# A four-layer transformer kernel on one core: a new order of work, and planned waits of TensorE filled to their full length

## The reference

```
L0  self attention over 1024 keys with rope and a mask, cross attention with a key mask, MLP with tanh-gelu
L1  self attention over 1024 keys, cross attention, MLP with tanh-gelu
L2  self attention in windows of 128 tokens, shifted by 64; cross attention over the 16 largest scores
    of each query (top-k); MLP with silu(a) * b
L3  self attention with rope, cross attention with rope, MLP with erf-gelu
```

## Time and profile before

| | us |
|---|---|
| median of 3 executions | 2982.82 |
| lowest, highest | 2969.13, 2983.83 |
| profiled execution, its own time | 2987.84 |
| span of the profiled execution | 2985.6 |
| TensorE busy | 2766.4 (93%) |
| VectorE busy | 1892.3 (63%) |
| ScalarE busy | 1421.3 (48%) |
| GpSimd busy | 714.7 (24%) |
| mean granted TensorE clock | 0.967 |

### The profile page before, as it was taken

How to read it: one execution, slowest core, us unless ns; L and a number is a source line. 1 busy time by engine, 2 the same in 40 slices (tenths; PEclk the granted TensorE clock), 3 DMA queues, 4 the chain that set the end, 5 groups by cost and what they waited for, 6 DMA issues and landing times.

```text
span 2985.6 us, 47850 instructions
## 1 busy us (share of the span) xinstructions
PE 2766.4 (93%) x15193; PEld 1377.7 (46%) x15249; DVE 1892.3 (63%) x4177; ACT 1421.3 (48%) x2579; POOL 714.7 (24%) x1063
## 2 busy tenths in 40 slices
PE   8999999999979998899988797899899999999899
PEld 5333444335535324344454565656554423324466
DVE  6887287642664882865554568667976684885621
ACT  3345535563433773566644343323124375676441
POOL 2101001131331110331224355533331000111420
PEclk9999999999989999999998898999899999999899
DMA  6252123322460322332166525531321232123631
GB/s 188 61 149 58 60 74 106 89 74 90 155 191 16 106 56 65 94 114 71 40 186 174 148 71 150 153 96 53 111 72 48 68 90 51 37 59 98 183 100 37
DMA packets 268153, 286.79 MB, mean 96 GB/s; under 512 B 70665, under 2 KB 207243, under 8 KB 267275
## 3 DMA queue, kind: packets, MB, share of 16 engines
q1 hardware_dynamic: 256651, 282.28, 32.3%
q0 software_dynamic: 11264, 1.46, 0.3%
HBM read 167.43 MB, written 114.72 MB: 95 GB/s over the span
## 4 chain that ended last, share of the span: by engine, by line
PE 69%; DVE 12%; DMA 9%; issue 5%; POOL 2%; SPq 2%; ACT 1%; DVEq 0%; ACTq 0%; POOLq 0%
PE ring_b L1420 11%; PE ring_c L1453 11%; PE ring_a L1376 10%; PE ring_b L1476 7%; PE ring_a L1488 7%; PE ring_b L1419 3%; PE ring_b L1333 3%; PE ring_a L1465 3%; DVE row_max L1739 2%; PE ring_a L1476 2%; DMA reciprocals<-scr_recip 2%; PE ring_b L1447 1%; DMA scr_out<-out_stage 1%; PE ring_a L1348 1%; PE ring_b L1408 1%
## 5 line engine op out<-in xcount | busy, mean ns | idle before, releaser
L1561 ACT ACTIVATE probs<-ring_b 128x512 f32<-128x512 f32 (+1 forms) x1728 | 919.2, 599 | 443.8 <-PE ring_b L1420 355.4
L1739 DVE TENSOR_REDUCE row_max<-ring_a 128x1 f32<-128x1024 f32 x512 | 602.0, 1218 | 178.5 <-PE ring_a L1376 177.7
L1420 PE MATMUL ring_b<-q_ring,k_ring 100*128 100x512 bf16 x1536 | 528.1, 381 | 15.0 <-ACT probs L1561 2.0
L1376 PE MATMUL ring_a<-k_ring,q_ring 96*128 96x512 bf16 x1536 | 452.9, 382 | 23.3 <-DVE row_max L1739 11.2
L1453 PE MATMUL ring_c<-probs,v_and_ones 128*17 128x512 f32 x3072 | 400.9, 598 | 2.3 <-ACT probs L1561 1.8
L1852 POOL CAST neg_max_parts<-neg_max 16x128 bf16<-16x128 f32 x112 | 35.6, 318 | 1344.9 <-ACT neg_max L1555 1142.9
L1736 DVE CUSTOM_DVE_ANT_0 w_mlp<-ring_a,w_mlp 128x1024 bf16<-128x1024 f32 x256 | 304.7, 1222 | 53.0 <-PE ring_a L1376 50.7
L1420 PEld LDWEIGHTS ring_b<-q_ring,k_ring 100*128 100x128 bf16 x1536 | 145.7, 97 | 347.9 <-issue 235.7
L1376 PEld LDWEIGHTS ring_a<-k_ring,q_ring 96*128 96x128 bf16 x1536 | 136.1, 98 | 252.3 <-issue 148.8
L1476 PE MATMUL ring_b<-h_feat,w_mlp 128*128 128x512 f32 x512 | 232.1, 600 | 4.1 <-issue 4.0
L1488 PE MATMUL ring_a<-w_mlp 128*128 128x256 f32 x1024 | 225.5, 380 | 2.1 <-issue 0.8
(11 more groups left out here) (144 smaller groups left out, 3514.8 us busy)
## 6 DMA issues: line engine op xcount, KB each, us to landing
q_ring<-scr_q SPq DMA_DIRECT2D x128, 384.0 KB, 4.3
scr_q<-split SPq DMA_DIRECT2D x64, 384.0 KB, 2.6
k_ring<-scr_k SPq DMA_DIRECT2D x64, 384.0 KB, 5.3
scr_q<-split SPq DMA_DIRECT2D x64, 256.0 KB, 3.0
scr_out<-out_stage SPq DMA_DIRECT2D x128, 128.0 KB, 2.4
scr_out<-out_stage SPq DMA_DIRECT2D x64, 256.0 KB, 2.7
h_feat<-scr_out SPq DMA_DIRECT2D x56, 256.0 KB
reciprocals<-scr_recip SPq DMA_DIRECT2D x56, 256.0 KB
```

The source lines that it names most:

```text
L1376: last = mm(ps[:, half * BLOCK:(half + 1) * BLOCK], q[0:PARTS, h, t * P:(t + 1) * P], k_view(g)[0:PARTS, h, half * BLOCK:(half + 1) * BLOC ...
L1420: last = mm(ps[:, :], k_view(g)[0:ROWS, h, s.kt * P:(s.kt + 1) * P], q[0:ROWS, h, q0:q0 + BLOCK], start=not g.masked, stop=True)
L1561: f(PT[0:n, s.pt, :], ps[0:n, :], ACT.Exp, **kw).then_inc(b_evac, 1)
L1739: v.tensor_reduce(NM[:, s.nm, s.u:s.u + 1], ps, AX.X, ALU.max).then_inc(a_evac, 1)
```

## The change

Four things in the planner change, nothing in the code that computes.

First, the ranks, REACH, DELAY, SECOND and LATER have other numbers, so that all five engines issue their steps in another order. Second, transfers are modelled otherwise: each has a time `dma` for its bytes, these queue on one line in the order of issue, and `lat` comes on top of it. Third, some durations are other ones: 2.1 for 1.7 us for the products with values in windows, 1.42 for 1.0 for the inverse root, 0.2 us more for the maxima's transfers. Fourth, fills take the whole planned wait and begin at 0.4 us of it instead of 0.8.

```diff
-            if rest > 0.8:
-                s["fill"] = int((rest - 0.3) * 0.7 / FILL_ONE)
+            if rest > 0.4:
+                s["fill"] = int(rest / FILL_ONE)
...
-            s["fill_o"], s["fill_on"], s["fill_ring"] = int((gap - 0.15) * 0.8 / FILL_ONE), self.count.get(o, 0), o
+            s["fill_o"], s["fill_on"], s["fill_ring"] = int(gap / FILL_ONE), self.count.get(o, 0), o
...
+        if "dma" in s:
+            self.line = max(self.line, at) + s["dma"]
+            end = max(end, self.line)
...
-    out=(0.9, -9, -8.6, -8.6),
+    out=(-12, -10, -8, -12),
...
-DELAY = (7.5, 20)
+DELAY = (7.5, 40)
...
-            s = yield do("root", [("POOL", 1.0)], after=[s], counts=["root_n"], l=l, i=i, b=b, blk=blk, of=s)
+            s = yield do("root", [("POOL", 1.42)], after=[s], counts=["root_n"], l=l, i=i, b=b, blk=blk, of=s)
...
-            s = yield do("load", [("SP", (0.9 if g.edge else 0.38) if cross else 0.82)], after=wr + [q_last, k_last], lat=4.6 if cross else 5.6, g=g, wr=wr,
+            s = yield do("load", [("SP", (0.9 if g.edge else 0.38) if cross else 0.82)], after=wr + [q_last, k_last], lat=3.2 if cross else 3.7, dma=1.1 if cross or g.k is None else 2.0, g=g, wr=wr,
...
-                    ph = [("PE", 1.7 if kind == "window" else 0.858), ("ACT", 0.487)]
+                    ph = [("PE", 2.1 if kind == "window" else 0.858), ("ACT", 0.487)]
...
-            r = yield do("recip_get", [("SP", 1.2 if st.akind == "window" else 0.6)], after=[put, e_last], lat=4.2, of=d, e=e, e_last=e_last, put=put, blk=blk)
+            r = yield do("recip_get", [("SP", 1.2 if st.akind == "window" else 0.6)], after=[put, e_last], lat=3.9, dma=0.67, of=d, e=e, e_last=e_last, put=put, blk=blk)
```

More of the change, by code:

```diff
@@ L107, in __init__ @@
         self.before = None
+        self.line = 0.0
     def take(self, name):
@@ L279 @@
 RANK = dict(
-    init=(8.1, -0.5, 4.1, 7.3),
-    mod=(-1.3, -7, -10, -12),
-    prep=(1, -12, 24, 1),
-    out=(0.9, -9, -8.6, -8.6),
[L284 to L295, removed]
-)
-REACH = dict(PE=0.0, ACT=0.1, DVE=0.0, POOL=0.2, SP=0.2)
-DELAY = (7.5, 20)
[L299 to L302, removed]
+    init=(11.3, -2.7, -2.7, 9.3),
+    mod=(-12, -12, -12, -9),
+    prep=(5, -9, 0, 10.4),
+    out=(-12, -10, -8, -12),
+    ctx=(2.5, 10.1, 7.7, 0.1),
+    load=(18.2, -1.2, 4.8, 0.8),
+    cross_f=(8.4, 0.8, 9.9, 7.9),
+    cross_s=(2.3, -2.2, -1.2, 2.3),
+    mlp=(7.1, 3.1, 1.1, 3.1),
+    self_f=(-5.4, 19.8, 16.8, 14.8),
+    self_pv=(18, 20, 16, 20),
+    self_s=(-2.8, 2.2, -2.8, 13.2),
+    tk=(-0.5, -1.5, -4.5, 5.5),
+    tk_s=(1.3, 11.7, -9.2, 1.3),
+    win_f=(-1.3, -9.3, -6.3, 1.7),
+    win_s=(4.7, 5.7, 6.7, -4.3),
+)
+REACH = dict(PE=0.0, ACT=0.2, DVE=0.1, POOL=0.1, SP=0.2)
+DELAY = (7.5, 40)
+SECOND = dict(init=-19, mod=-9, prep=-5, out=6, ctx=-10, load=-12, cross_f=6,
+              cross_s=11, mlp=-20, self_f=2, self_pv=6, self_s=-9, tk=12, tk_s=-12,
+              win_f=-1, win_s=24)
+LATER = (-1, -12.5, -40, -19.5)
 FILL_ONE = 0.11
@@ L340, in mods @@
             _, last, _ = yield ("get", "MODS")
-            s = yield do("mod_load", [("SP", 0.9)], after=[last], lat=3.5 if n == 0 else 10.0 if n == 2 else 3.2, l=l, i=i, last=last, n=n)
+            s = yield do("mod_load", [("SP", 0.9)], after=[last], lat=2.3 if n == 0 else 8.0 if n == 2 else 2.3, dma=1.3, l=l, i=i, last=last, n=n)
             s = yield do("mod", [("PE", 1.68), ("DVE", 0.41)], after=[s], ring="a", l=l, i=i, n=n)
@@ L357, in weights @@
                 rel.append(s)
-        s = yield do("weight", [("SP", 0.5)], after=rel, lat=us, name=name, l=l, b=b, rel=rel, uses=uses)
+        s = yield do("weight", [("SP", 0.5)], after=rel, lat=us, dma=dma, name=name, l=l, b=b, rel=rel, uses=uses)
         p.raise_flag((name, l, b), s)
@@ L369, in context_weights @@
                 rel.append(last)
-            s = yield do("weight", [("SP", 0.5)], after=rel, lat=5.0, name="ckv", l=l, b=0, rel=rel, uses=l + 1)
+            s = yield do("weight", [("SP", 0.5)], after=rel, lat=3.0, dma=1.34, name="ckv", l=l, b=0, rel=rel, uses=l + 1)
             p.raise_flag(("ckv", l), s)
@@ L386, in row_load @@
         slot, last, uses = yield ("get", "ROW")
-        s = yield do("row", [("SP", 0.47)], after=[last], lat=5.3, l=l, i=i, which=which, slot=slot, last=last, uses=uses)
+        s = yield do("row", [("SP", 0.47)], after=[last], lat=4.2, dma=0.37, l=l, i=i, which=which, slot=slot, last=last, uses=uses)
         return s
@@ L408, in split_chain @@
         p.give("RAW", raw, d)
-        w = yield do("scratch", [("SP", 1.57)], after=[d], lat=2.8, of=s, done=d)
+        w = yield do("scratch", [("SP", 1.57)], after=[d], lat=2.2, dma=0.96 if ck else 2.2, of=s, done=d)
         p.give("SPLIT", sp, w)
@@ L494, in gate_thread @@
             slot, last, uses = yield ("get", "WO")
-            w = yield do("wo_load", [("SP", 0.45)], after=[last], lat=5.0, l=l, i=i, slot=slot, last=last, uses=uses)
+            w = yield do("wo_load", [("SP", 0.45)], after=[last], lat=2.4, dma=0.74, l=l, i=i, slot=slot, last=last, uses=uses)
         else:
@@ L503, in gate_thread @@
                     free.append(s)
-            w = yield do("w2_load", [("SP", 0.45)], after=[last] + free, lat=5.6, l=l, i=i, last=last, uses=uses, free=free)
+            w = yield do("w2_load", [("SP", 0.45)], after=[last] + free, lat=3.6, dma=2.9, l=l, i=i, last=last, uses=uses, free=free)
             slot = 0
@@ L511, in gate_thread @@
             _, last, uses = yield ("get", "GW")
-            gw = yield do("gw_load", [("SP", 0.43)], after=[last], lat=6.0, l=l, i=i, last=last, uses=uses)
+            gw = yield do("gw_load", [("SP", 0.43)], after=[last], lat=4.1, dma=0.74, l=l, i=i, last=last, uses=uses)
             _, g_last, _ = yield ("get", "G")
@@ L700, in products @@
                 p.give("PC", 0, s)
-            w = yield do("put", [("SP", 0.33 if st.cross else 1.13)], after=[s], lat=2.3, of=s, g=unit.g, ost=ost, uses=o_uses)
+            w = yield do("put", [("SP", 0.33 if st.cross else 1.13)], after=[s], lat=2.2, dma=0.34 if st.cross else 0.68, of=s, g=unit.g, ost=ost, uses=o_uses)
             p.give("OST", ost, w)
```

24 lines of the change are left out of this document (12 added, 12 removed).

## The result

The changed kernel takes 2928.35 us (2925.78 to 2930.36), the kernel before 2981.65 us in the same comparison. The ratio is 0.9829, with an interval of 0.9801 to 0.9858: 1.7% faster. The forecast was 2948 us, with a range of 2900 to 2996. The profiled execution spans 2925.4 us, 60.2 less than the 2985.6 of before.

What follows compares the result with a forecast made beforehand. TensorE bounds the kernel, busy 2766.4 of 2985.6 us; idle time and fills make 481.7 us. Order -40, fills +30 and clock -25 sum to -35 us: 2952.8 us profiled, 2948 us as a median, range 2900 to 2996.

Steps and rivals of the forecast that it cites:

- Part 1, the order: New order of steps on all engines: less waiting of TensorE, -40 us, bounds -27 and -78.
- full shortfall: Cover missing against the chains' quickest runs, over 244 TensorE steps: 258.9 us before, 205.3 after, a difference of 53.6.
- the cover: Summed time of TensorE products between a chain's start on other engines and the first TensorE step needing its result.
- my five kinds: Kinds of counted steps: top-k, 'pv' to 'out', projections, 'out' and 'down' to transposes, maxima.
- Part 2: Fills to full length on TensorE, 1075 more: costs +30 us, between zero and 66.
- part 3: TensorE's clock falls to half speed less often: -25 us, bounds 0 and -72.
- bound of 66 us: Most that lengthened fills could cost: 120 us of added length less the idle time that stood behind fills.
- signs for reading the profile: Expected: clock 0.975 to 0.98, TensorE idle 100 to 130 us, fills some 400 us, no L2 transpose wait over 3 us.
- One sign: TensorE's fills plus idle time: above 482 us the fixed fills have won; if they grow, the prediction is wrong.
- the second rival: Fixed fills eat the gain, costing more than order and clock bring together (65 us): 3009 or 3022 us; slower side, 15%.
- The third rival: A wash: the planner's single line of transfers puts landings and fills at wrong places, about 0, 2983 us; 20%.

Runs made afterwards that it cites:

- e2: The changed kernel with the old rule for fills (0.7 and 0.8 of the wait, from 0.8 us; 1757 fills): 2926.66 us, ratio to before 0.9807.
- e4: The changed kernel, so the new order, without any fills: 2946.55 us, ratio to before 0.9867.
- e3: The kernel before, so the old order, without any fills: 3005.64 us, ratio to before 1.0071.
- e1: The kernel before with the change's rule for fills (whole planned wait, from 0.4 us; 3152 fills): 2988.74 us, ratio to before 1.0015.
- e7: The changed kernel with every fill 1.3 times as long as the planned wait (3880 fills): 2984.98 us.
- e6: The changed kernel with the old RANK, REACH, DELAY, SECOND and LATER, keeping its new durations, line of transfers and full fills: 3008.43 us, ratio to before 1.0094.
- e11: The changed kernel with five tables from a search replaying orders under scattered landing times, and the old rule for fills: 2921.74 us, ratio to before 0.9805.
- e12: A second result of the same search, from another random start, in the changed kernel with the old rule for fills: 2920.17 us, ratio to before 0.9796.

## Why the prediction was right

Part 1, the order, was forecast at -40 us with bounds of -27 and -78, and measured at -57 (e2) and -59 (e4 against e3). That the order brings the gain was right, and the term was a third too small. The full shortfall was 53.6 us, close to what came. But its parts are not the parts that the traces show. Between e3 and e4 the idle time before the norm's transposes fell by 24 us, where the cover said 8.0. Before the top-k transposes it fell by 10, where the cover said 26.6 and I took half, 13.3: that cut was right in size, and the place in L2 above shows VectorE as the limit for which I made it. Before first passes and top-k scores together it fell by 27, where the cover said 14.3. And before 'up', which stands in none of my five kinds, it rose by 22 (both rings). So the full sum is a good count of the whole in part by luck. Why the norms gained three times their cover is not shown.

In time, most of the gain had been made by the end of L2. The last 'down' of L2 ends where the transposes behind it begin, in before:

```profile
2346.68 4.91 PE L1488 MATMUL ring_a<-w_mlp 128*128 128x256 f32 x22
2351.43 0.82 PE L1298 MATMUL ring_b<-ident_f,x_norm 128*128 128x128 f32 x6
```

and in the changed kernel:

```profile
2272.72 5.13 PE L1492 MATMUL ring_a<-w_mlp 128*128 128x256 f32 x23
2277.68 1.04 PE L1302 MATMUL ring_b<-ident_f,x_norm 128*128 128x128 f32 x8
```

That is 74 us earlier. The last 'down' of L1 ends 43 us earlier, that of L0 10 us later, and the end only 60 us earlier, so some of the work has moved behind L2. The order has a second gain that I had not put into its term: with it the slow loss is 8 to 13 us smaller at the same rule for fills.

Part 2 was forecast at +30 and part 3 at -25, together +5. By the split of e1 against before they are +39 and -40, together -1 (the profiled spans differ by -4.9, of which -4 are neither), while the medians say +5 (2983.47 to 2988.74; the interval of the ratio, 0.9998 to 1.0032, just holds no change). In the new order the two are +42 and -34. Both terms were too small by 9 to 15 us, and that the two misses cancel is luck; nothing in the working ties them. The bound of 66 us for fills that are too long was a true upper bound, and e7 shows that beyond the full length more than half of each is lost.

The misses then: the order by 17 to 19 us, and the two terms that cancel. The median came out 20 us below the forecast, which is the order's miss. Of my signs for reading the profile, the granted clock (forecast 0.975 to 0.98) was 0.988, the idle time (100 to 130) 115.1 and the fills (some 400) 376.7; the longest wait for a norm in L2 was 1.5 us. One sign was wrong, and I had given it twice: if fills and idle time together exceed 482 us, the fixed fills have won, and if they grow, I am wrong. They grew to 491.8, and the kernel was 53 us faster. The sign leaves out the products that ran slowly: 50 us of the gain appear there. Taken alone, the full fills did not win anything, so the second rival had the right mechanism and the wrong outcome; its condition, fills costing more than order and clock bring together, was far from met (42 for the fills, against 52 of waits by the order and 47 of slow loss in all).

The third rival, that a single line of transfers sends the order wrong, is not borne out for the change as a whole. But e6 shows that the line with the old ranks loses 20 us against the old model. The Trainium skill (DMA: Bandwidth & Descriptors, "Queues, rings and completion order") says that completions are not first in, first out per issuing engine. No run here puts a model of that kind beside the line; what the runs show is that tables chosen with the line gave an order 57 us shorter.

Holding the clock was worth nothing here beyond the old rule, as the fills that hold it cost as much: 0.922 without fills, 0.967 with the old rule and 0.985 with full ones, at 3005.64, 2983.47 and 2988.74 us. The Trainium skill (TensorE: Matmul & The Clock Gate, "Why this matters for your kernels") says that long idle gaps halve the clock. The traces agree: in the old order the half-speed stretches last 466 us without fills, 199 with the old rule and 92 with full ones.

## What to carry to other kernels

For an order that is fixed in the program, count for each chain of work the products that stand between its start and its first user, and set them against the chain's quickest run in the trace. The shortfall told the rough size of each change of order here to within about 20 us, and its sign where it was 50 us or more (and for e6, forecast at 8); for e11 and e12, 3 and 6 us, it told nothing. It is a sum to rank orders by, not a list of which waits will shrink. Fill planned waits, but not beyond their length: from the old rule to the full length the time was the same in the new order, and 1.3 times the length cost 57 us. A clock near 1 and a busy share of 96% are then no sign of a good kernel: compare the real products and the waits apart.

## What I had not expected

Fills as a whole were worth 20 us of 3000 in both orders (2983.47 for 3005.64 us, 2926.66 for 2946.55), though without them the clock falls to 0.922. The 1873 fills of the old order lower the slow loss by 103 us and raise the waits by 111 in the table, some 86 of it real by my estimate.

Full-length fills instead of the old rule were neutral to 5 us in both orders. Three rules in the new order, 1757 fills, 0.85 of the wait and 2948 fills, gave 2926.66, 2929.42 and 2928.35 us, while the clock went from 0.978 to 0.988.
